# First layer of a two-layer recurrent block: the division by a seeded Newton iteration, a new order, and three projections as fp16 passes

## The reference, cut to what matters

```python
xn = layernorm(x)
xm = xn * time_mix + shift(xn) * (1 - time_mix)
k, v, r = xm @ Wk.T, xm @ Wv.T, xm @ Wr.T
k   = exp(minimum(k, 60));  kv = k * v
wkv = causal_decay_conv(kv);  wk = causal_decay_conv(k) + 1e-9
s   = (sigmoid(r) * wkv / wk) @ Wo.T
h   = relu(s0 * [xn, -xn] @ sign(k0)) * 2
h   = relu(s1 * h @ sign(k1)) * 2
x   = x + s * silu(s2 * h @ sign(k2))
```

## Time and profile before

| | us |
|---|---|
| median of 3 executions | 673.99 |
| lowest, highest | 672.09, 675.5 |
| the profiled execution | 672.1 |
| its span, first to last instruction | 670.3 |
| PE busy | 629.5 (94%) |
| DVE busy | 601.0 (90%) |
| ACT busy | 511.4 (76%) |
| POOL busy | 280.1 (42%) |

### The profile page before, as it was taken

How to read it: one execution, slowest core, us unless ns; L and a number is a source line. 1 busy time by engine, 2 the same in 40 slices (tenths; PEclk the granted TensorE clock), 3 DMA queues, 4 the chain that set the end, 5 groups by cost and what they waited for, 6 DMA issues and landing times. The chain is left out here.

```text
span 670.3 us, 9285 instructions
## 1 busy us (share of the span) xinstructions
PE 629.5 (94%) x2714; PEld 304.2 (45%) x2714; DVE 601.0 (90%) x1406; ACT 511.4 (76%) x794; POOL 280.1 (42%) x275
## 2 busy tenths in 40 slices
PE   4779999999999998799999999999999999999986
PEld 2334444444444443344545444454444544444442
DVE  4999999999999999988988988898898899889856
ACT  2846666666666665889988898898888889899886
POOL 6556777777777765222123032122313303221220
PEclk9999999999999999999999999999999999999999
DMA  7331000000000000000000000000000000000000
GB/s 178 109 94 31 1 0 1 1 0 1 0 2 1 0 1 1 1 0 1 16 1 17 17 4 14 16 17 0 17 17 1 17 17 17 0 18 17 0 17 32
DMA packets 10770, 11.65 MB, mean 17 GB/s; under 512 B 4800, under 2 KB 6288, under 8 KB 10720
## 3 DMA queue, kind: packets, MB, share of 16 engines
q1 hardware_dynamic: 9744, 10.73, 5.3%
q0 software_dynamic: 112, 0.33, 0.1%
q10 hardware_dynamic: 864, 0.00, 0.1%
HBM read 6.87 MB, written 4.19 MB: 16 GB/s over the span
## 5 line engine op out<-in xcount | busy, mean ns | idle before, releaser
L1150 PE MATMUL bank<-arena,w 128*128 128x512 f16 x640 | 148.6, 379 | 4.1 <-DVE arena L774 4.1
L1150 PE MATMUL bank<-arena,dnT 128*128 128x512 f32 x288 | 138.6, 592 | 0.0
L435 POOL TENSOR_TENSOR arena<-arena 128x512 f32<-128x512 f32 x48 | 59.7, 1271 | 137.6 <-ACT arena L590 137.6
L650 ACT ACTIVATE arena<-bank,xinv 128x512 f32<-128x512 f32 x144 | 94.4, 693 | 24.9 <-PE bank L1150 24.6
L1150 PEld LDWEIGHTS bank<-arena,w 128*128 128x128 f16 x640 | 62.5, 98 | 78.3 <-issue 10.1
L482 ACT ACTIVATE arena<-bank 128x512 f16<-128x512 f32 x96 | 53.8, 606 | 35.8 <-PE bank L1150 35.8
L425 POOL TENSOR_TENSOR arena<-arena 128x512 f32<-128x512 f32 x16 | 16.8, 1050 | 140.6 <-DVE arena L1011 140.6
L1150 PEld LDWEIGHTS bank<-arena,dnT 128*128 128x128 f32 x288 | 53.7, 191 | 35.9 <-issue 24.4
L1150 PE MATMUL bank<-arena,wsqT 128*128 128x512 f32 x128 | 64.6, 609 | 5.3 <-DVE arena L783 5.3
L1020 DVE SCALAR_TENSOR_TENSOR arena<-bank,cws,arena 128x506 f32<-128x506 f32 (+1 forms) x96 | 67.1, 740 | 1.1
L774 DVE SCALAR_TENSOR_TENSOR arena<-bank,arena 128x512 f16<-128x512 f32 x96 | 60.3, 671 | 2.4 <-ACT arena L482 1.2
(11 more groups left out here) (221 smaller groups left out, 1492.6 us busy)
## 6 DMA issues: line engine op xcount, KB each, us to landing
x_all<-in_L_attn_x SPq DMA_DIRECT2D x16, 256.0 KB, 2.6
out<-x_all SPq DMA_DIRECT2D x16, 256.0 KB, 2.0
up_n<-in_L_ffn_routed_up SPq DMA_DIRECT2D x1, 512.0 KB, 3.7
dn_n<-in_L_ffn_routed_down SPq DMA_DIRECT2D x1, 512.0 KB, 5.3
wx<-in_L_attn_W_x SPq DMA_DIRECT2D x1, 288.0 KB, 2.9
k_u<-in_L_ffn_k POOLq DMA_DIRECT2D x1, 256.0 KB, 5.8
w_in<-in_L_attn_W_in SPq DMA_DIRECT2D x1, 256.0 KB, 2.7
k_u<-in_L_ffn_k SPq DMA_DIRECT2D x1, 128.0 KB, 6.1
```

The costliest lines, as they stand in the source:

```text
L435: g.tensor_tensor(prod[:, c, :], act[:, c + 1, :], gate[:, :], ALU.mult).then_inc(sem["b_actp"], 1)
L650: a.activation(act[:, c, :], up_bank(f, c)[:, :], ACT.Gelu, scale=xinv[:, I_UP:I_UP + 1]).then_inc(sem["b_act"], 1)
L1150: return nc.tensor.matmul(ps, lhsT, rhs, start=start, stop=stop)
```

## The change

1. The division. `rec` was 1/`wk` by DVE's reciprocal in two halves of 256 columns. Now ACT makes a seed: exp of the scaled integer bits of `wk`. POOL multiplies `ya` = wk * rec (semaphore `a_t1`), DVE does the first Newton step into `rec` (`first_step`), DVE multiplies again (`second_product`), POOL multiplies `ysr` by `rec` (`a_q`), and DVE's `second_step` makes `ya`. The sign that is left over goes into the new constant `c3[:, 3:4]`.
2. The projections. Wk, Wv and Wr are split into an fp16 high and low half (`sqH`, `sqL`, made once in `scales`), and so is `xm`: high half by ACT (`xmh`), low half by DVE (`xml`). Each product is three fp16 passes from group 2 on; groups 0 and 1 stay fp32 (`plain`). The scales of exp and tanh, and of `kv`, become values read from SBUF.
3. The order. On PE the turn of `sg` goes behind the second hidden chunk. On DVE the four low halves and `gp` go ahead of the scan of `kv`. One more maximum of weights is taken (`I_SQ`).

The diff, cut to its core (the scans of `kv`, which stood ahead of the four low halves, now follow `gp`):

```diff
@@ POOL, layer0 @@
+                    pool.wait_ge(sem["a_rec"], m + 1)
+                    g.tensor_tensor(ya[:, :], wk[:, :], rec[:, :], ALU.mult).then_inc(sem["a_t1"], 1)
                     for j in range(POOLED):
                         g.tensor_tensor(hl[:, 1, j, :], relu[:, j, :], hh[:, 1, j, :], ALU.subtract)
-                    pool.wait_ge(sem["a_rec"], m + 1)
+                    pool.wait_ge(sem["a_r1"], m + 1)
                     pool.wait_ge(sem["a_ysr"], m + 1)
-                    g.tensor_tensor(ya[:, :], ysr[:, :], rec[:, :], ALU.mult).then_inc(sem["a_y"], 1)
+                    g.tensor_tensor(ysr[:, :], ysr[:, :], rec[:, :], ALU.mult).then_inc(sem["a_q"], 1)
...
                 if has(f):
+                    after(pool, sem["a_y"], f)
                     pool.wait_ge(sem["a_wkc"], f + 1)
@@ ACT, layer0 @@
+                    if not plain(f):
+                        actv.wait_ge(sem["a_xm"], f + 1)
+                        a.activation(xmh[:, :], xm[:, :], ACT.Copy).then_inc(sem["a_xmh"], 1)
+                if has(m):
+                    actv.wait_ge(sem["a_wk"], m + 1)
+                    after(actv, sem["a_q"], m)
+                    a.activation(rec[:, :], wk[:, :].bitcast(mybir.dt.int32), ACT.Exp, scale=SEED_SCALE,
+                                 bias=seedb[:, :]).then_inc(sem["a_rec"], 1)
...
-                    a.activation(ek[:, :], b_K[:, :], ACT.Exp).then_inc(sem["a_ek"], 1)
+                    a.activation(ek[:, :], b_K[:, :], ACT.Exp, scale=unscale(f)).then_inc(sem["a_ek"], 1)
@@ DVE, new functions @@
+                v.scalar_tensor_tensor(rec[:, :], ya[:, :], NEWTON, rec[:, :], ALU.subtract, ALU.mult)
+                v.tensor_tensor(ya[:, :], wk[:, :], rec[:, :], ALU.mult).then_inc(sem["a_t2"], 1)
+                dve.wait_ge(sem["a_q"], n + 1)
+                v.scalar_tensor_tensor(ya[:, :], ya[:, :], 2.0, ysr[:, :], ALU.add, ALU.mult)
@@ DVE, layer0 @@
+                    if not plain(f):
+                        dve.wait_ge(sem["a_xmh"], f - 1)
+                        v.tensor_tensor(xml[:, :], xm[:, :], xmh[:, :], ALU.subtract).then_inc(sem["a_xml"], 1)
...
-                    v.reciprocal(rec[:, 0:N // 2], wk[:, 0:N // 2])
+                    first_step(m)
+                    second_product(m)
...
-                    v.tensor_tensor(kv[:, :], ekm[:, :], b_V[:, :], ALU.mult).then_inc(sem["a_kv"], 1)
+                    v.scalar_tensor_tensor(kv[:, :], b_V[:, :], unscale(f), ekm[:, :], ALU.mult, ALU.mult)
+                if has(m):
+                    second_step(m)
...
-                    v.reciprocal(rec[:, N // 2:], wk[:, N // 2:]).then_inc(sem["a_rec"], 1)
                     low(1, m, 2)
                     low(1, m, 3)
...
+                if has(f) and f != 0:
+                    low(0, f, 0)
+                    low(0, f, 1)
+                    low(0, f, 2)
+                    low(0, f, 3)
+                if has(m):
+                    v.scalar_tensor_tensor(gp[:, :], thf[:, :], 1.0, b_F[:, :], ALU.add, ALU.mult)
@@ DVE, scales (once) @@
+                halves(sqH[:, :], sqL[:, :], wsqT[:, 0:3, :].rearrange(flat), col(wsc, I_SQ)).then_inc(sem["sq_ready"], 1)
@@ PE, layer0 @@
+                    mm(ps[:, :], sqH[:, w], xmh[:, :], True, False)
+                    mm(ps[:, :], sqL[:, w], xmh[:, :], False, False)
+                    if i == 0:
+                        pe.wait_ge(sem["a_xml"], f - 1)
+                    return mm(ps[:, :], sqH[:, w], xml[:, :], False, True)
```

More of the change, by code:

```diff
@@ L18 @@
 WK_EPS = 1e-9
+LOG2 = math.log(2.0)
+SEED_SCALE = -LOG2 / 2 ** 23
+SEED_BIAS = LOG2 * (127 - 0.043)
+NEWTON = 2.00045
 K_CAP = 60.0
@@ L60, in build @@
     GV = RC - GP
-    I_IN, I_UP, I_RW, I_WX, I_DT, I_CW, I_CB = range(7)
-    NSC = 7
+    I_IN, I_UP, I_RW, I_SQ, I_WX, I_DT, I_CW, I_CB = range(8)
+    NSC = 8
     XC_S, C_FAC, B_FAC, D_FAC = range(4)
@@ L84, in build @@
         epsc = sb("epsc", [P, J])
+        seedb = sb("seedb", [P, 1])
         wsq = sb("wsq", [P, 4, P])
@@ L129, in build @@
         inv = sb("inv", [P, NSC])
-        xinv = sb("xinv", [P, 3])
+        xinv = sb("xinv", [P, 4])
+        half_sq = sb("half_sq", [P, 1])
+        mixs = sb("mixs", [P, 2])
+        sqH = sb("sqH", [P, 3 * P], F16)
+        sqL = sb("sqL", [P, 3 * P], F16)
+        xmh = sb("xmh", [P, N], F16)
+        xml = sb("xml", [P, N], F16)
         bnd = sb("bnd", [P, 2])
@@ L306, in build, with plain, unscale @@
         CONV_DONE = [CONV_AT[k, TAPS - 2] for k in range(IC)]
+        def plain(n):
+            return isinstance(n, int) and n < 2
+        def unscale(n):
+            return 1.0 / XS if plain(n) else xinv[:, I_SQ:I_SQ + 1]
         def xs_of(n):
@@ L529, in layer0 @@
                     actv.wait_ge(sem["a_r"], f + 1)
-                    a.activation(thr[:, :], b_RX[:, :], ACT.Tanh, scale=0.5).then_inc(sem["a_thr"], 1)
+                    a.activation(thr[:, :], b_RX[:, :], ACT.Tanh, scale=0.5 / XS if plain(f) else half_sq[:, :]).then_inc(sem["a_thr"], 1)
                     if f != 0:
@@ L562, in last_hidden @@
             def last_hidden():
+                m = G - 1
+                actv.wait_ge(sem["a_wk"], m + 1)
+                actv.wait_ge(sem["a_q"], m)
+                a.activation(rec[:, :], wk[:, :].bitcast(mybir.dt.int32), ACT.Exp, scale=SEED_SCALE,
+                             bias=seedb[:, :]).then_inc(sem["a_rec"], 1)
                 high(1, G - 1, 0)
@@ L791, in layer0 @@
                         row_stats(f + 1)
+                    if not plain(f):
+                        dve.wait_ge(sem["a_xmh"], f - 1)
+                        after(dve, sem["a_r"], f)
+                        v.tensor_tensor(xml[:, :], xm[:, :], xmh[:, :], ALU.subtract).then_inc(sem["a_xml"], 1)
+                    if ahead:
                         dve.wait_ge(sem["a_xn"], f + 1)
@@ L831, in layer0 @@
                     largest()
-                if has(f):
-                    dve.wait_ge(sem["a_kv"], f + 1)
-                    after(dve, sem["a_wkv"], f)
-                    for s in range(SEQ):
-                        last = v.tensor_tensor_scan(Pv[:, s, 1:], dec[:, :], kv[:, s * T:(s + 1) * T], 0.0,
-                                                    ALU.mult, ALU.add)
-                    last.then_inc(sem["a_scanV"], 1)
                 if has(f) and f != 0:
@@ L847, in layer0 @@
                     v.scalar_tensor_tensor(gp[:, :], thf[:, :], 1.0, b_F[:, :], ALU.add, ALU.mult).then_inc(sem["a_gp"], 1)
+                if has(f):
+                    dve.wait_ge(sem["a_kv"], f + 1)
+                    after(dve, sem["a_wkv"], f)
+                    for s in range(SEQ):
+                        last = v.tensor_tensor_scan(Pv[:, s, 1:], dec[:, :], kv[:, s * T:(s + 1) * T], 0.0,
+                                                    ALU.mult, ALU.add)
+                    last.then_inc(sem["a_scanV"], 1)
+                if has(m):
                     dve.wait_ge(sem["a_gp"], m + 1)
@@ L871, in col, with halves @@
                 return t[:, i:i + 1]
+            def halves(high, low, src, factor):
+                link(v.tensor_scalar(high, src, factor, None, ALU.mult))
+                return v.scalar_tensor_tensor(low, src, factor, high, ALU.mult, ALU.subtract)
             def scales():
@@ L1226, in layer0 @@
                     hidden1(m, 0)
+                if has(m):
+                    hidden1(m, 1)
                 if has(t):
@@ L1232, in layer0 @@
                     turn_back(b_RX).then_inc(sem["a_sgT"], 1)
-                if has(m):
-                    hidden1(m, 1)
                 if has(f):
```

63 lines of the change are left out of this document (39 added, 24 removed).

## The result

The changed kernel takes 710.86 us (median; 710.26 to 711.65), the kernel before beside it 673.95: 1.055 times as long, 95% interval 1.052 to 1.058. The prediction said 706.3. The profiled execution took 711.65 with a span of 709.7; before had 670.3, so 39.4 us of span are to be found. Only layer 0 has them: from the first convolution product of layer 1 to the end both kernels take 396.1.

The account below looks back on a forecast made before the run. DVE was taken to bound the kernel at 15.52 a body; thirteen bodies at +2.02 (26.3), 4.5 for body 1, body 15 and tail, and 1.5 once made +32.3, 704.4, then 1.9 to the median: 706.3, range 688 to 717.

Parts of the forecast that it names:

- the exclusion: DVE instructions with two SBUF inputs and whole-tile POOL instructions exclude each other; DVE coming second ends 0.55 after POOL.
- The rival that had no exclusion: The new forms do not hold each other: body 14.79, execution 664, faster; chance 0.12.
- PE's saving: Three fp16 passes at 0.70 replace an fp32 product at 1.01: -0.93 a body, hidden behind DVE.
- Steps (a) to (f): Body from POOL's wkv to DVE's scan of keys, with holds: xml ends 2.54, first step 5.25, second product 6.74.
- Step (g): POOL's centring 9.77 to 10.81, first key scan ends 11.41, POOL's xn 12.24, second scan 12.79.
- Step (h): Body's end: four low and gp 2.99, scan of kv 1.16, sg 0.67; next xm at 17.54.
- The start: Body 1 at 1.5 for division steps without xml; once 1.5 for a maximum and two halving passes.
- The tail: Body 15 and the tail's three division steps, with the norm of layer 1 among them: 1.5 each.
- DVE gets in first: First step slips in ahead of POOL's low 0: +1.4 a body, execution 697; chance 0.13.
- Holds add up: Holds cost the other's whole length or kv scans are met, +0.8 a body, 717; clock fall counted in; chance 0.10.

Follow-up runs that it names:

- e_pool: Changed kernel with POOL's two low halves put behind its products wk * rec and ysr * rec; 684.74 us, ratio 1.016.
- e_psum: Changed kernel with the four new DVE instructions reading their second input from PSUM, not SBUF, in groups 0 to 14; 684.45 us, ratio 1.016.
- e_tail: Changed kernel with only the last group's division, in the tail, by the two old reciprocals; 707.58 us, ratio 1.052.
- v_cap: Kernel before with the keys' cap moved from DVE to ACT, second reciprocal ahead of kv, kv scans at the body's end; 667.29 us, ratio 0.992.
- e_ekm: Kernel before with the keys' cap moved from DVE to POOL behind its low halves, kv behind the second reciprocal; 714.94 us, ratio 1.062.
- v_cap_scan: Kernel before with the keys' cap on ACT and second reciprocal ahead of kv, kv scans left behind the key scans; 703.97 us, ratio 1.046.

## Why the prediction came out as it did

**What bounds it, and the exclusion: right.** DVE sets the body, PE's shorter projections are hidden, and the new DVE instructions shut out POOL's passes and are shut out by them: three of the four in the body read above, the second step only in `e_pool` (0.86). `e_psum` takes the cause away without touching the count of instructions, `e_pool` without touching DVE, and in both the first step falls from 1.63 to 0.69. The rival that had no exclusion falls by that. PE's saving was too large at -0.93 a body: I had divided busy times by counts. From start to start an fp32 product of the kernel before costs 0.86 and three fp16 passes 0.65, so three products save 0.6. As all of it is hidden, nothing hung on this.

**Steps (a) to (f): right in order and cause, late by 0.1 to 0.4.** Against step and time from `xm`: `ysr` ends 2.12 (predicted 1.99), `xml` 2.67 (2.54), POOL's product 3.80 (3.60), `low` 0 4.92 (4.70), the first step 5.47 (5.25), `low` 1 6.48 (6.19), second product 7.03 (6.74), POOL's second product 8.16 (7.80), capped keys 8.44 (8.08), second step starts 9.14 (8.79). Two small terms make this up. POOL starts `wkv` 0.15 after the scans end; I gave that 0.07. And a held POOL product ends 1.13 after DVE (174.59 to 175.72, 178.95 to 180.08) and the shorter `low` 1.01 after it (177.39 to 178.40), where I had a pass's time less 0.21, 1.06 and 0.94; the overlap is 0.14, as on DVE's side (0.69 - 0.55). My 0.21 was one row's, with an end worked out of a pair. The Trainium skill (SBUF — State Buffer, Who interferes with whom) says the later instruction is blocked for the whole of the other. Which instructions are blocked agrees in the rows shown here; the time is the whole less these 0.14.

**Step (g): partly wrong.** I had POOL's centring still running when the first key scan starts (9.77 to 10.81), the pass behind it (`xn`) held by that scan until 12.24, and the second scan held by `xn`. The centring ran 9.57 to 10.73 and was over before the scans, so `xn` (L391, 10.87 to 11.91) came ahead of the first scan and held it (it ends 12.46, again 0.55 later); the second scan met nothing (0.66). By luck the price is the same: one scan held, +0.84 for a predicted +0.81. **Step (h)**: the next `xm` at 17.75, predicted 17.54; 0.21 of 13 bodies is 2.7 us of the 7.1 that the sum was short.

**The start: a little short.** Body 0, body 1 and what is done once were 3.0 in the sum and came to 4.0. Body 0 (+1.3) had only one new maximum (0.5) in the sum. In body 1 the fp16 halves of the weights took 0.4 and 0.6, but the rest is again holds. DVE's timeline there:

```profile
31.30 1.49 DVE L870 TENSOR_SCALAR arena<-arena 128x512 f32<-128x512 f32 x1
...
37.54 1.16 DVE L930 TENSOR_SCALAR adiag<-ident,amx 8x8 f32<-8x8 f32 x1
...
44.32 1.21 DVE L955 TENSOR_TENSOR bnd<-bnd,amax 128x1 f32<-128x1 f32 x1
```

The same three take 0.36, 0.22 and 0.16 in body 1 of the kernel before; here each has a POOL pass beside it. One of the small ones was held in the kernel before too (1.05), so the list is not all gain. The granted clock was at half for 3.4 us from 26.7, where before had it full, but DVE waits for nothing in this body, so no cost of it shows.

**The tail: mis-sized.** This is the largest part of the error. Body 15 and the tail were 1.5 each, 3.0, worked out as the steps' price plus what is held behind them. They measured 6.3; the 3.3 missing are nearly half of the 7.1. The cost of the body was carried over to a place where DVE's new step has nothing in front of it to cover POOL's norm steps (2.15 idle), PE has no other work while it waits (4.91), and its clock then falls. `e_tail` gives 4.9 of the 6.3 back in its profiled execution. I had counted a fall of the clock as part of a rival, for the bodies; there, with PE idle 2.65 of 17.75, it stayed at 1.00. In the tail it came.

**The rivals.** "DVE gets in first" failed by 0.08: POOL's `low` starts at 175.68, the first step at 175.76. "Holds add up", with a clock fall, is where the tail went, but the bodies did not.

## What to carry to other kernels

Price a VectorE pass that reads two SBUF tiles by what GpSimd runs at that moment, not by its row where it ran alone: in these runs 0.69 becomes up to 1.63, ending 0.55 after GpSimd. A pass with one input in PSUM kept its 0.67 to 0.75 beside GpSimd. Before moving work, list, for every VectorE pass behind it that reads two SBUF tiles, which GpSimd pass it will now meet; the cheapest places are where GpSimd waits for that very result, and those beside its small steps. And price the last, uncovered instance of a loop's work by itself.

## What the runs showed of the hardware that was not expected

A small size does not by itself protect an instruction: a VectorE TENSOR_SCALAR on 128x7 took 1.17 us for 0.16, because it had to see GpSimd's 128x512 pass out, and ended 0.02 after it. One on 128x1 beside the same pass (L896 of `v_cap`) kept its 0.15. And the meetings feed back: one instruction moved to GpSimd (`e_ekm`) made the steady body 2.4 and 4.1 us longer by turns, and two scans in another place (`v_cap_scan` against `v_cap`) 3.1 and 3.9, the last two kernels having the same instructions on every engine. The exponential of integer bits on ScalarE took 0.71, as its form with a scale from SBUF does.
